# One list of rows per expert, and results added into the output by 39 indirect DMAs

## The chip, the cores and the metric

The kernel runs on one core of a Trainium2 chip. The time is device microseconds (us) of one execution, the median of several. PE is TensorE, DVE is VectorE, ACT is ScalarE, POOL is GpSimd, SP is SyncE, which here only issues DMAs. A "q" behind a name (SPq) is that engine's instruction queue.

## The reference, cut to what matters

All tensors are float32: x is (4, 512, 512), the context (4, 1024, 512), so there are 2048 tokens. First a gated linear attention, then a mixture of 8 experts in which each token takes its best two.

```python
x = x + xattn(layernorm(x), ctx, Wq, Wg, bg, Wkv, Wo)
x = x + ffn(layernorm(x), Wr, We, be)

def ffn(x, Wr, We, be):
    logits = einsum('bsd,de->bse', x, Wr)
    w, sel = top_k(logits, 2)
    w = softmax(w)
    gate = einsum('bsk,bske->bse', w, one_hot(sel, 8))
    out = 0
    for e in range(8):
        out = out + gate[..., e:e+1] * (x @ We[e] + be[e])
    return out
```

## The kernel before, in words

Every engine has its own program; semaphores order them. Every product of two float32 matrices is made of three float32r passes (`three`, L1105: high by high, high by low, low by high), 12 matmuls for 128 rows by 512 by 512.

**Attention.** Batches b = 0 to 3 go one after the other through `queries(b)` and `keys(b + 1, b)`, whose orders are the lists KEYS and QUERIES (L233 to L249). The router's work of batch b (transposes "z", logits "L", ranks "K") is spread over the keys of b + 1. `residual` writes x2 = x + attention, and SP stores x2 of batches 0 to 2 in DRAM (`store_x2`). The normalised rows are scattered by POOL (`scatter`, L490) with two indirect DMAs of 128 rows into xs, one region per expert.

**Groups and tiles.** There are two groups of tokens, batches 0 to 2 and batch 3, each with its own regions, its own plan and its own padding of the last tile of each expert. A tile is 128 rows of one expert. Group 0 has 31 tiles and group 1 has 15, always 46; tiles beyond the real ones repeat the last. `plan` (L957) works out for each tile its expert and first row.

**A tile.** SP loads the rows (`load_tile`, L359, two slots, xs_raw). PE transposes them (`turn_m`, L1173), ACT copies the high part (`high_m`), DVE subtracts for the low part (`low_m`), PE multiplies (`expert`, L1223), DVE adds the expert's bias (`copy_y`, L1021) and ACT stores the tile in the DRAM tensor y. START (L295) fixes the order: the transposes of tile m + 1 stand before the product of tile m, and between the first ten tiles stand the router's steps of batch 3. The split weights of experts 1 to 7 are loaded from DRAM by SP, 2 MB each (`load_halves`); those of 4 to 7 come when attention gives the space back.

**The end.** When all tiles of a group are stored, POOL gathers for each 128 tokens their two rows of y (`gather`, L602), DVE multiplies them by the router's weights and adds them to x2 (`combine`, L1028), and ACT stores the result. Twelve combines run between the tiles of group 1; the four of batch 3 come after the last tile.

## Time and profile before

| | us |
|---|---|
| median of 3 runs | 601.4 (600.34 to 603.24) |
| the profiled execution, its own time | 605.42 |
| its span in the profile | 603.9 |
| PE busy in it | 546.0 |

The span runs from the first to the last instruction; the execution's own time is 1.52 us more. Start and length of instructions below are in us from the span's start.

### The profile page before, as it was taken

How to read it: one execution, taken by the hardware profiler on the slowest of the kernel's cores; microseconds unless marked ns; L12 is line 12 of the kernel's file. 1: busy time of each engine (PE TensorE's matmuls, PEld its weight loads, DVE VectorE, ACT ScalarE, POOL GpSimd, SP SyncE). 2: the span in 40 equal slices, each digit the busy share in tenths (PEclk: the TensorE clock that was granted, in tenths of full speed). 3: DMA queues.
4: the chain of work that ended last, by engine and by line, in shares of the span. 5: the costliest groups of instructions: out<-in, count | busy, mean ns of one | idle time of the engine just before them, and what ended most of it. 6: DMA issues, size and time to landing. Idle time of an engine off the chain costs nothing.

```text
span 603.9 us, 12871 instructions
## 1 busy us (share of the span) xinstructions
PE 546.0 (90%) x4192; PEld 443.9 (74%) x4193; DVE 323.3 (54%) x857; ACT 187.8 (31%) x340; POOL 170.9 (28%) x200
## 2 busy tenths in 40 slices
PE   6999999999999999999999999968799999958850
PEld 4778788878778887877887878856577888846640
DVE  4573367274357556337737537744466444437643
ACT  5455323434422333532343443321111111111100
POOL 4433453315540403632131430010130000156313
PEclk9999999999999999999999999998899999989885
DMA  8912533613541433363062258599566579589946
GB/s 280 363 39 106 174 140 112 238 71 125 192 170 40 162 118 106 144 199 112 0 245 71 79 198 316 198 384 415 189 216 187 163 236 296 160 266 314 380 172 188
DMA packets 44478, 114.18 MB, mean 189 GB/s; under 512 B 5008, under 2 KB 5008, under 8 KB 43536
## 3 DMA queue, kind: packets, MB, share of 16 engines
q1 hardware_dynamic: 24240, 57.43, 27.7%
q0 software_dynamic: 11264, 39.85, 18.9%
q10 hardware_dynamic: 8928, 16.26, 7.1%
q8 instruction: 32, 0.52, 0.4%
q14 instruction: 14, 0.11, 0.1%
HBM read 66.86 MB, written 46.66 MB: 188 GB/s over the span
## 4 chain that ended last, share of the span: by engine, by line
PE 82%; DMA 7%; issue 4%; DVE 3%; another core or an unknown queue 1%; ACT 1%; POOL 1%; SPq 0%; POOLq 0%; DVEq 0%; ACTq 0%
PE pj L1110 23%; PE pj L1112 22%; PE pj L1111 22%; PE tp L1102 5%; DMA khat<-xs 5%; PE tp L1177 3%; PE pj L1197 2%; PE kvb L1169 2%; PE pj L1119 1%; DMA wraw<-in_L_xattn_Wkv_dram 1%; DMA num<-y,gidx 1%; DVE R L809 1%; DVE R L818 1%; ACT R L648 0%
## 5 line engine op out<-in xcount | busy, mean ns | idle before, releaser
L1110 PE MATMUL pj<-R 128*128 128x512 f32 x448 | 184.4, 412 | 4.9 <-DVE R L818 4.3
L1112 PE MATMUL pj<-R 128*128 128x512 f32 x448 | 176.6, 394 | 0.0
L1111 PE MATMUL pj<-R 128*128 128x512 f32 x448 | 175.8, 392 | 0.0
L1110 PEld LDWEIGHTS pj<-R 128*128 128x128 f32 x448 | 84.9, 189 | 21.6 <-DVE R L818 4.5
L1112 PEld LDWEIGHTS pj<-R 128*128 128x128 f32 x448 | 84.6, 189 | 19.1
L1111 PEld LDWEIGHTS pj<-R 128*128 128x128 f32 x448 | 85.1, 190 | 15.2
L1110 PE MATMUL pj<-R,aux 128*128 x184 | 78.7, 428 | 9.5 <-DVE aux L822 6.6
L1111 PE MATMUL pj<-R,aux 128*128 x184 | 73.5, 399 | 0.0
L1112 PE MATMUL pj<-R,aux 128*128 x184 | 73.5, 399 | 0.0
L728 ACT CAST aux<-tp 128x512 fp32r<-128x512 f32 x46 | 26.9, 586 | 128.8 <-PE tp L1177 101.9
L818 DVE TENSOR_TENSOR R<-tp,R 128x512 fp32r<-128x512 f32 x64 | 43.8, 684 | 21.2 <-ACT R L648 21.2
L883 DVE SCALAR_TENSOR_TENSOR khat<-buf,khat 128x512 f32<-128x512 f32 x32 | 25.1, 784 | 53.6 <-ACT buf L687 47.2
L1110 PEld LDWEIGHTS pj<-R,aux 128*128 128x128 f32 x184 | 35.9, 195 | 18.7 <-issue 12.6
L495 POOL DMA_INDIRECT xs<-normed,xidx x16 | 15.9, 992 | 100.4 <-DVE xidx L871 97.9
L608 POOL DMA_INDIRECT qhat<-y,gidx x16 | 16.0, 997 | 98.8 <-issue 78.7
L502 POOL TENSOR_TENSOR rstd<-rstd,mhalf 128x1 f32<-128x1 f32 (+1 forms) x20 | 13.4, 669 | 104.9 <-DVE rstd L836 104.8
L822 DVE TENSOR_TENSOR aux<-tp,aux 128x512 fp32r<-128x512 f32 x46 | 31.7, 689 | 19.6 <-ACT aux L728 17.7
L1112 PEld LDWEIGHTS pj<-R,aux 128*128 128x128 f32 x184 | 35.7, 194 | 7.9
L1177 PE MATMUL tp<-ident,khat 128*128 128x128 f32 x184 | 28.9, 281 | 13.3 <-DMA khat<-xs 13.2
L1111 PEld LDWEIGHTS pj<-R,aux 128*128 128x128 f32 x184 | 36.1, 196 | 6.1
L648 ACT CAST R<-tp 128x512 fp32r<-128x512 f32 x64 | 37.7, 589 | 8.5 <-PE tp L1102 8.0
L1177 PEld LDWEIGHTS tp<-ident,khat 128*128 128x128 f32 x184 | 22.6, 143 | 19.1 <-DMA khat<-xs 11.8
(159 smaller groups left out, 677.0 us busy)
## 6 DMA issues: line engine op xcount, KB each, us to landing
we_halves<-aux POOLq DMA_DIRECT2D x14, 1024.0 KB, 5.1
R<-we_halves SPq DMA_DIRECT2D x7, 2048.0 KB, 11.1
khat<-xs SPq DMA_DIRECT2D x46, 256.0 KB
buf<-in_ctx_dram SPq DMA_DIRECT2D x15, 512.0 KB, 4.2
wraw<-in_L_ffn_We_dram POOLq DMA_DIRECT2D x14, 512.0 KB, 6.7
y<-kvbd ACTq DMA_DIRECT2D x23, 256.0 KB
y<-zeros ACTq DMA_DIRECT2D x23, 256.0 KB
wraw<-in_x_dram SPq DMA_DIRECT2D x4, 1024.0 KB, 8.1
```

The source lines that it names most:

```text
L495: nc.gpsimd.indirect_dma_start(out=xs_dram[g][:, :], out_offset=bass.IndirectOffsetOnAxis(ap=xidx[:, t, j:j + 1], axis=0), in_=xn[t], in_o ...
L608: nc.gpsimd.indirect_dma_start(out=yg[slot][j], out_offset=None, in_=y_dram[g][:, :], in_offset=bass.IndirectOffsetOnAxis(ap=gidx[:, slot, ...
L648: nc.scalar.copy(dst, src).then_inc(SEMS["h_" + kind], 1)
L728: nc.scalar.copy(xsT_hi[:, slot, :, :], tp[slot][:, :, :]).then_inc(MOE["h_m"], 1)
L818: nc.vector.tensor_tensor(lo, tp_bank("l_" + kind, i)[:, :, :], hi.bitcast(F32), ALU.subtract).then_inc(SEMS["l_" + kind], 1)
L822: nc.vector.tensor_tensor(xsT_lo[:, slot, :, :], tp[slot][:, :, :], xsT_hi[:, slot, :, :].bitcast(F32), ALU.subtract).then_inc(MOE["l_m"], 1)
L883: nc.vector.scalar_tensor_tensor(khat[:, i % 2, :], expk[:, i % 2, :], 1.0, khat[:, i % 2, :], ALU.min, ALU.add).then_inc(SEMS["khat"], 1)
L1102: last = nc.tensor.transpose(bank[:, k, :], src[:, k * P:(k + 1) * P], ident[:, :])
L1110: nc.tensor.matmul(bank[:, :], s_hi(k), m_hi(k), start=(k == 0), stop=False)
L1111: nc.tensor.matmul(bank[:, :], s_hi(k), m_lo(k), start=False, stop=False)
L1112: last = nc.tensor.matmul(bank[:, :], s_lo(k), m_hi(k), start=False, stop=(k == KT - 1))
L1177: last = nc.tensor.transpose(tp[slot][:, k, :], xs_raw[:, slot, k * P:(k + 1) * P], ident[:, :])
```

## The change

- One group: xs has one region per expert for all 2048 tokens. A row has 528 elements: 512 values, 8 gates (the router's weight for each expert, 0 for those not chosen), the token's number and a flag for padding.
- 39 tiles in all. The first M0 = 17 are full tiles of batches 0 to 2 in the order of experts (`plan_full`); the other 22 (`plan_rest`) are first tiles that are not needed, which point to four spare blocks of zero rows, and then the remaining tiles, again by expert. The trip count is always 39.
- No y in DRAM, no gathers, no combines. x2 of all four batches is stored in the output itself. Each tile's result gets its bias on DVE, is multiplied by the gate on ACT (`scale_y`), and POOL adds its 128 rows to the output with one indirect DMA with compute_op add (`add_rows`). There are four result buffers, as many as adds can be in flight.
- Two experts' tiles can hold the same token, tiles of one expert cannot. `tile_alone` is 16 for the first tile of an expert's run (and for tile 17) and 0 for the others; it is added to the values that `add_rows` waits for. With 16 the three adds before must have landed, with 0 only those from which the buffers were taken over.
- Padding rows point to tokens of the first 256 which the expert doesn't have (`mark_pads`, `find_pads`, PE step "C"), with values and gates of 0.
- Tile loads have four slots instead of two. SP loads the halves of an expert one after the other, each after the one before has landed. The biases are loaded in part by ACT.
- The loops over tiles, and DVE's loop over batches, are written out.

```diff
-    GROUP_TILES = ((B - 1) * TT, TT)
-    TILES = [2 * n + E - 1 for n in GROUP_TILES]
+    M0 = (2 * (B - 1) * L - E * (P - 1) + P - 1) // P
+    M_ALL = PAIRS // P + E - 1
+    XS, YS = 4, 4
...
+            def load_tile(m):
+                row = sp.value_load(tile_row[0:1, m:m + 1], min_val=0, max_val=E * ROWS + (YS - 1) * P)
+                if m >= XS:
+                    sp.wait_ge(MOE["t_m"], mth(m - XS))
+                    sp.wait_ge(paid, m - XS + 1)
+                sp.dma_start(xs_raw[:, m % XS, :], xs_dram[bass.ds(row, P), :]).then_inc(xs_loaded[m % XS], 16)
             def load_halves(e):
+                sp.wait_ge(wx_stored, 16 * 2 * e)
+                sp.wait_ge(we_ready, 16 * e)
+                sp.dma_start(R[:, 2 * e:2 * e + 2, :, :].rearrange("p a k d -> p (a k d)").bitcast(F32), wx_dram[e, :, :]).then_inc(we_ready, 16)
...
             sp.wait_ge(planned, 1)
-            sp.wait_ge(zeroed, 1)
-            with sp.Fori(0, E) as e:
-                pad(0, e, zeros[:, :])
             for t in range(TT):
                 sp.wait_ge(scattered[t], 32 * (B - 1))
-            load_tile(0, 0, 0)
-            load_tile(0, 1, 1)
-            sp.wait_ge(SEMS["qhat"], nth("qhat", B - 1, G - 1))
-            for e in range(E):
-                sp.dma_start(be_all[:, e, :], be[e:e + 1, :].broadcast_to((P, D))).then_inc(be_loaded, 16)
+            for m in range(XS):
+                load_tile(m)
             sp.wait_ge(SEMS["g"], nth("g", B - 1, TT - 1))
             load_halves(4)
             load_halves(5)
-            load_tile(0, 2, 0)
+            load_tile(XS)
+            store_x2(B - 1)
             sp.wait_ge(SEMS["wo"], nth("wo", B - 1, TT - 1))
-            load_tile(0, 3, 1)
             load_halves(6)
-            load_tile(0, 4, 0)
+            load_tile(XS + 1)
             load_halves(7)
...
+            def add_rows(m):
+                slot = m % YS
+                pool.wait_ge(y_scaled, m + 1)
+                if m >= 1:
+                    alone = pool.value_load(tile_alone[0:1, m:m + 1], min_val=0, max_val=16)
+                    for d in range(1, min(m, YS - 1) + 1):
+                        pool.wait_ge(added[(m - d) % YS], alone + 16 * ((m - d) // YS + 1))
+                nc.gpsimd.indirect_dma_start(out=out_rows[:, :], out_offset=bass.IndirectOffsetOnAxis(ap=out_idx[:, m % (2 * YS):m % (2 * YS) + 1], axis=0),
+                                             in_=y_sb[slot], in_offset=None, compute_op=ALU.add).then_inc(added[slot], 16)
...
+            def scale_y(m):
+                act.wait_ge(MOE["y_copied"], mth(m))
+                nc.scalar.activation(y_sb[m % YS], y_sb[m % YS], ACT.Identity, scale=w_sel[:, m % (2 * YS):m % (2 * YS) + 1]).then_inc(y_scaled, 1)
...
+            def pay(m):
+                e = dve.value_load(tile_expert[0:1, m:m + 1], min_val=0, max_val=E - 1)
+                nc.vector.tensor_scalar(w_sel[:, n:n + 1], row[:, bass.ds(e + GATES, 1)], 1.0, None, ALU.mult)
+                nc.vector.scalar_tensor_tensor(out_idx[:, n:n + 1], pad_token[:, bass.ds(e, 1)], row[:, PADDED:PADDED + 1],
+                                               row[:, TOKEN:TOKEN + 1], ALU.mult, ALU.add).then_inc(paid, 1)
+            def copy_y(m):
                 dve.wait_ge(MOE["m_done"], mth(m))
+                if m >= YS:
+                    dve.wait_ge(added[m % YS], 16 * (m // YS + 1))
+                nc.vector.tensor_tensor(y_sb[m % YS], pj[m % 2][:, :], be_all[:, bass.ds(chosen[m], 1), :].rearrange("p a d -> p (a d)"), ALU.add)
```

`plan_rest` runs in three parts after copy_y of tiles 9, 10 and 11: 14, 13 and 7 DVE operations, each waiting for the one before; the arrays over tiles and experts have 176 elements. `mark_pads` follows after tiles 12 to 14 with 6, 8 and 8 operations. On PE, step "C" after tile 15 is 16 matmuls with one column each.

## Rows read from the trace of the kernel before

**Rows 1.** The page: busy us of each engine, share, instructions.
```profile
PE 546.0 (90%) x4192; PEld 443.9 (74%) x4193; DVE 323.3 (54%) x857; ACT 187.8 (31%) x340; POOL 170.9 (28%) x200
```
**Rows 2.** Windows: start:end length, busy us (instructions) per engine, clock, DMA share, GB/s.
```profile
397.70:451.20 53.50, 41.30 (x337) 31.77 (x336) 25.66 (x104) 9.68 (x20) 7.75 (x10) 0.90 0.78 302
465.00:485.00 20.00, 20.00 (x104) 16.69 (x103) 8.90 (x13) 3.83 (x7) 0.00 (x0) 1.00 0.51 157
529.00:543.00 14.00, 7.82 (x39) 6.08 (x38) 4.99 (x9) 1.21 (x3) 7.97 (x8) 0.87 0.83 273
543.00:583.00 40.00, 35.02 (x152) 27.50 (x150) 27.74 (x49) 5.25 (x9) 14.87 (x14) 0.92 0.87 309
583.00:603.90 20.90, 0.00 (x0) 0.00 (x0) 6.91 (x11) 0.00 (x0) 8.37 (x8) 0.52 0.57 176
```
**Rows 3.** Chain that ended last, in order of time: start, us, what.
```profile
395.29 14.66 DMA khat<-xs
416.47 10.52 DMA khat<-xs
468.25 0.44 PE tp L1177 x4
471.43 0.44 PE tp L1177 x4
534.58 6.08 another core or an unknown queue
550.94 7.76 DMA khat<-xs
582.48 2.19 DMA y<-zeros
595.13 4.64 DMA num<-y,gidx
```
**Rows 4.** Timeline of SP's issues, from 387 to 395.
```profile
387.00 1.91 SPq L363 DMA_DIRECT2D khat<-xs  x2
393.45 1.07 SPq L376 DMA_DIRECT2D R<-we_halves  x2
```
**Rows 5.** Timeline of PE: transposes of tiles 1 and 2; wait before a product.
```profile
397.68 0.60 PE L1177 MATMUL tp<-ident,khat 128*128 128x128 f32 x4
409.99 1.11 PE L1177 MATMUL tp<-ident,khat 128*128 128x128 f32 x4 [8.09 <-DMA khat<-xs]
462.06 0.49 PE L1110 MATMUL pj<-R,aux 128*128 x1 [0.50 <-DVE aux L822]
```
**Rows 6.** Timeline of DVE: plan of group 1, its first and last operations.
```profile
455.31 0.16 DVE L970 SCALAR_TENSOR_TENSOR pad_row<-iota,run 128x8 int32<-128x8 f32 x1
456.73 0.69 DVE L822 TENSOR_TENSOR aux<-tp,aux 128x512 fp32r<-128x512 f32 x1
458.95 0.28 DVE L984 TENSOR_TENSOR qhat<-tile_t,tb 128x120 f32<-128x120 f32 x1
461.13 0.69 DVE L822 TENSOR_TENSOR aux<-tp,aux 128x512 fp32r<-128x512 f32 x1
```
**Rows 7.** Groups by line: names, shapes, count, busy us, mean ns of one.
```profile
L728 ACT CAST aux<-tp 128x512 fp32r<-128x512 f32 x46 | 26.9, 586 | 128.8 <-PE tp L1177 101.9 <-remote 10.3 <-issue 9.2
L658 ACT ACTIVATE normed<-gate,shift,rstd 128x512 f32<-128x512 f32 x8 | 6.5, 816 | 7.8 <-POOL shift L503 7.8
L1119 PE MATMUL pj<-wr_sb,qhat 128*32 128x8 f32 x512 | 7.0, 179 | 0.0
```
**Rows 8.** Timeline of POOL and DVE: gathers of the first combines, and at the end.
```profile
527.68 0.97 POOL L608 DMA_INDIRECT qhat<-y,gidx  x1 [0.30 <-issue]
532.87 0.75 DVE L1032 SCALAR_TENSOR_TENSOR wraw<-qhat,wts,wraw 128x512 f32 x1 [1.63 <-DMA qhat<-y,gidx]
586.85 0.95 POOL L608 DMA_INDIRECT qhat<-y,gidx  x1 [0.30 <-issue]
```
**Rows 9.** The page's DMA issues: KB each, us to landing.
```profile
R<-we_halves SPq DMA_DIRECT2D x7, 2048.0 KB, 11.1
```

More of the change, by code:

```diff
@@ L297, in xattn_moe_kernel @@
         START += [("K", "", 1)] + tiles(6) + [("L", "", 3)] + tiles(7) + [("K", "", 2)] + tiles(8) + [("K", "", 3)]
-        START += tiles(9) + tiles(10) + tiles(11) + tiles(12)
-        LOOP1 = 13
-        N_COMB = GROUP_TILES[0]
-        LOOP2 = M_ALL - N_COMB
-        assert (FIRST[1] - LOOP1) % 2 == 0 and N_COMB == 12 and LOOP2 % 2 == 0 and LOOP2 > FIRST[1]
-        def res_tile(c):
-            return x2r[:, bass.ds(c, 1), :].rearrange("p a d -> p (a d)")
+        for m in range(9, M_ALL):
+            START += tiles(m) + ([("C", "", 0)] if m == M0 - 2 else [])
+        START.remove(("T", "m", M_ALL))
         block = stack.enter_context(nc.Block())
@@ L598, in _ @@
-            halves_in(7)
-            for t in range(TT):
-                scatter(1, last, t)
-            def gather(g, c, slot):
-                pool.wait_ge(gidx_done, c + 1)
-                pool.wait_ge(combined, c + 1)
-                passed()
-                for j in range(2):
-                    nc.gpsimd.indirect_dma_start(out=yg[slot][j], out_offset=None, in_=y_dram[g][:, :],
-                                                 in_offset=bass.IndirectOffsetOnAxis(ap=gidx[:, slot, j:j + 1], axis=0)).then_inc(gathered[slot], 16)
@@ L628, in _ @@
+            for step, kind, i in START:
+                if step == "M":
+                    if i == M0 + 2:
+                        pool.wait_ge(planned, 2)
+                    if i >= 2:
+                        add_rows(i - 2)
+                elif step == "K":
+                    scatter(last, i)
+            add_rows(M_ALL - 2)
+            add_rows(M_ALL - 1)
+            for s in range(YS):
+                pool.wait_ge(added[s], 16 * ((M_ALL - 1 - s) // YS + 2))
         @block.scalar
@@ L998, in plan @@
-                link(nc.vector.tensor_reduce(ys, tok, AX_X, ALU.add))
-                nc.vector.scalar_tensor_tensor(ys, ys, float(P), rank[:, q0:q0 + N, :].rearrange("p q j -> p (q j)"), ALU.mult, ALU.add).then_inc(planned, 1)
-                dve.wait_ge(planned, g + 1)
+                nc.vector.tensor_scalar(tile_expert[:, m0:m0 + T], tile_e[:, 0:T], 0.0, None, ALU.max)
+                link(nc.vector.tensor_tensor(more, big, over(nt[:, 0:E], T), ALU.mult))
+                link(nc.vector.tensor_reduce(tile_b[:, 0:T], more, AX_X, ALU.add))
@@ new lines, in mark_pads @@
+            def mark_pads():
+                tokens = token[:, :].rearrange("p (t e) -> p t e", e=1).broadcast_to((P, 2, E))
+                link(nc.vector.tensor_scalar(early_run[:, :], early_run[:, :], -1.0, float(2 * P), ALU.mult, ALU.add))
+                link(nc.vector.tensor_tensor(member_place[:, :, :], early[:, :, :], over(early_run[:, :], 2), ALU.add))
+                link(nc.vector.tensor_tensor(early[:, :, :], tokens, early[:, :, :], ALU.subtract))
+                link(nc.vector.tensor_tensor(early[:, :, :], early[:, :, :], member_place[:, :, :], ALU.subtract))
+                link(nc.vector.scalar_tensor_tensor(list_place[:, :, :], early_members[:, :, :], 0.0, early[:, :, :], ALU.is_equal, ALU.mult))
+                link(nc.vector.tensor_tensor(list_place[:, :, :], list_place[:, :, :], member_place[:, :, :], ALU.add))
+                dve.wait_ge(x2_stored, 16 * B + 16)
+                yield
+                for t in range(2):
+                    for e in range(E):
+                        last = nc.vector.tensor_scalar(marks[:, t, e, :], place_p[:, :], list_place[:, t, e:e + 1], None, ALU.is_equal)
+                    last.then_inc(pads_marked, 1)
+                    yield
@@ L1042, in _ @@
                     low_m(i, i % 2)
+                    pay(i)
                 elif step == "M":
-                    copy_y(i, i % 2, i // 2)
+                    copy_y(i)
+                    if 9 <= i < 12:
+                        next(planning, None)
+                    if 12 <= i < 15:
+                        next(marking, None)
                 elif step == "L":
@@ L1047, in _ @@
                 elif step == "K":
[L1048 to L1076 removed]
+                    rank_two(LAST, i, pj[2 + i % 2])
+                elif step == "C":
+                    find_pads(pj[2])
         @block.tensor
```

496 lines of the change are left out of this document (228 added, 268 removed).

## The prediction, made before the changed kernel was run

> **What bounds the kernel now.** I read the page's busy times first, then windows, the chain of waits in order of time, and last the timelines of the stretches where the chain leaves PE. PE is busy for 546 of 603.9 us and no other engine for more than 323 [rows 1], so time is won only where PE has less to do or waits less. In the tile stage the chain returns to the transposes every 3.18 us (468.25 to 471.43) [rows 3]: 0.45 for the transposes, 2.73 for 12 products, PE busy throughout at full clock [rows 2]. The stage is a whole: from 397.68, where tile 1 is turned [rows 5], PE works until DVE takes the last tile at 581.8, 184.1 us later. Its work there is 45 x 3.18 + 2.73 = 145.8 for the tiles and some 5 for the router: four transposes like those of [rows 5] at 0.60, four logits steps at 7.0 / 16 = 0.44 [rows 7], and ranks, put at 0.2 each. So 33.3 us of it are not work, and the reader should see where they lie. Early, two tile loads of 256 KB take 14.66 and 10.52 us in the chain [rows 3], because each stands behind halves of 2 MB on SP's queue that were issued just before [rows 4]; PE's clock falls to a mean of 0.90 there [rows 2]. Nine tiles from 397.7 to 451.2 should cost 28.6 + 5 and cost 53.5: 19.9 lost. Late, at 534.58 the chain names an unknown source for 6.08 us, just where ACT, DVE and POOL enter their next loop round, and at 550.94 a tile load takes 7.76 beside gathers [rows 3]; the windows from 529 to 583 have a clock of 0.87 and 0.92 [rows 2]. That is most of the other 13. After the last product comes a tail of 22 us without PE: store, eight gathers one behind the other, a last landing of 4.64, two combines, a store [rows 2, 3].
>
> **The change, part by part.** The sum is made against the profiled execution: span 603.9, and 1.52 around it.
>
> *Seven tiles fewer.* 46 becomes 39: 7 x 3.18 = 22.3 us off PE. The same three-pass product stays. From 397.68: 38 x 3.18 + 2.73 = 123.6, router 5.0, step C 16 one-column products and a wait, 0.8 (nearest row: a logits step of 32, 0.44; bound 0.2 to 2). That makes 129.4, or 527.1. I assume that attention before it runs as now: DVE gains one small operation in `pick_two` and loses one in `rank_two`, under PE's cover; the written out batch loop could give back a us or two at loop edges, which I put at 0 (bound -3 to +2).
>
> *Early loads.* Tiles 0 to 3 are loaded when the plan is ready, some 15 us before the halves of expert 4, since the eight padding stores and their wait are gone. What is late next? Halves 4 can go at 387 instead of 393.45, since no bias loads stand before them [rows 4]. Each pair of halves now waits for the one before; with 7 us each (2 MB at the 302 GB/s of the first window [rows 2]) to 11.1 (the median to landing [rows 9]) halves 7 lands between 415 and 431. Tile 4 lands behind halves 5, tile 5 behind 6, tile 6 behind 7. PE turns tile 4 at about 410, tile 5 at 413, tile 6 at 417. So something like 0 to 14 us is left of the 19.9. In addition SP now stores 1 MB of x2 there and ACT's bias loads come late (the last at about 402), for which copy_y(0) waits, and all of DVE behind it. I take 4.
>
> *Planning on DVE.* Before, 6 and 9 linked operations (455.31 to 456.73 and 458.70 to 461.13) cost PE 0.50 once [rows 5, 6]. Now there are 14, 13 and 7, those over all tiles of 176 elements where 120 took 0.28 [rows 6]: about 3.1, 3.8 and 1.8 us. DVE's own work per tile is two passes of 0.6 and now two small operations and a register load, 1.9 of 3.18, so three tiles take it 14.4 us against 9.5. With a slack of 0.7 this stalls PE by some 4 (bound 1 to 6). The marks behind tiles 12 to 14 are 1 to 1.5 us each and fit.
>
> *The adds.* They are the part that the trace doesn't show. ACT's `scale_y`, 0.82 like the activation in [rows 7], and `high_m`, 0.59, are 1.4 of 3.18: hidden. POOL needs about 0.96 for an indirect DMA and spaces them by 1.25 [rows 8]. y's stores and the gathers of [rows 3] go away. Open is L, the time from an add's issue to its landing. From below: a direct store of 256 KB lands in 2.19 [rows 3]. From above: the slowest 256 KB load beside other traffic, 14.66 [rows 3]. Nearest: a gather, 4.64 at the end [rows 3] and 532.87 - 527.68 = 5.2 under load [rows 8]. An add reads its target and writes it back, so a gather and then a write is 4.64 + 2.19 = 6.8 if they don't overlap. I take L = 6. DMA has room: a load and a store per tile make a share of 0.51 [rows 2]; a second read beside it should give 0.7 to 0.9.
>
> What L costs follows from the waits. The routing is fixed by the inputs; worked out with the reference, the tiles by expert are 3, 2, 3, 2, 2, 2, 3 in the first 17 (experts 0 to 6), then four unneeded ones, then 1, 2, 2, 3, 2, 3, 2, 3. No expert has more than 112 of the first 256 tokens, so no further tile waits. Within a run of n tiles the adds follow 1.25 apart if POOL is behind, between runs one whole L passes. The last eight runs thus take 8 L + 10 x 1.25 at least, against 18 x 3.18 = 57.2 us of PE; an add can go 2.1 us after its product. Counted from tile 21, whose add itself waits for tile 20's, the last landing is 9 L - 42.6 us after the unstalled end of PE; counted over all 16 runs and with the early and planning losses, 16 L - 104. At least it is L + 2.1. The larger counts; whether it shows as PE waiting for a result buffer (copy_y waits for the add four back) or as tail is the same. For L = 5 it is 7.1, for 6 11.4, for 7 20.4, for 8 29.4, for 10 56.
>
> *Tail.* So the 22 us become 11.4, and 0.6 for the end of the program. I allow 2 for clock and issue losses behind the stalls above (the late ones of [rows 3] lose their cause, gathers and loop rounds; bound 0 to 6).
>
> Sum: 527.1 + 4 + 4 + 2 + 11.4 + 0.6 = 549.1 span, 550.6 execution against 605.4, that is 54.8 less. The profiled execution is 4.0 above the median of the runs; taken from 601.4, this leaves 546.6 us.
>
> **The rivals.**
>
> A. *An add is no slower than a gather*, L = 4.7: the chain between experts vanishes and the floor of 6.8 counts, 4.6 less: 542. For it: reading the target overlaps with the data read. Against it: the chip must have the target's value before it can write. The gather row gives 4.64 with nothing else running [rows 3]. The Trainium skill, page "DMA: Bandwidth & Descriptors", section "Anatomy of one DMA — SWDGE (gpsimd) path", gives 2.0 us plus bytes at 436 GB/s, an estimate of 2.6 for 256 KB; the page "Collectives: The Full Stack", section "The bandwidth ceiling: the fold count and why AG ≠ RS ≠ AR", says that an add in the DMA costs two source reads, so half the rate, an estimate of 3.2, and with POOL's 0.96 4.2. By these the sum would be 542 too. This trace's gather is a us above the same estimate without the second read, so I lean to the longer side.
>
> B. *Adds are slow under load*, L = 8: the chain of expert changes sets the end, 18 more: 565. For it: loads beside software gathers took 7.76 [rows 3]. Against it: that was beside a gather every 1.7 us, now there is one in 3.18. PE would be seen waiting for copy_y, on an add.
>
> C. *The early jam stays.* The bytes in front of tiles 4 to 6 are the same 8 MB and 1 MB more, and the serial halves add a landing each. If 20 us are lost as now instead of 4: 563. Against it: four tiles in hand are 13 us of work.
>
> D. *Slower than before.* L above 10.6: then max(9 L - 42.6, 16 L - 104) is over 65 and eats all 54.8. At L = 11.5 the time is 546.6 + 80 - 11.4 = 615. The place is the wait for `added` in `add_rows`, at each change of expert. It can also come from more waits than I count: were every add to wait for the one before, 39 x 6 + 2.1 - 134.6 = 101 us would follow, 636. For it: nothing here shows an add; 128 rows of 2 KB, 8 on each of 16 queues, each read and written back in turn at 1 us or more would do it. Against it: gathers show no such cost per row.
>
> E. *It doesn't do what it says*: the early and late gains are real but PE's tiles grow, since each load has 3% more bytes and DMA is near full. PE has four tiles in hand, so I give this no time of its own.
>
> **How the numbers follow.** Forecast (L between 5 and 7) 0.50, A 0.12, B 0.14, C 0.10, D 0.11, and 0.03 that what is gained and lost comes within 0.5% of nothing, about what a measurement of this kernel can tell from no change. The first four are faster: 0.86; slower 0.11. The predicted time is 547. The forecast's own range is 537 to 558. Ends for 8 in 10: below, A with no losses early and in planning, 542 - 8 = 534; above, it takes in B and C and L up to about 9 (40.3, 29 more: 576), with the other bounds half used 10 more: 586.
>
> **What would show it.** Right: 39 x 16 products and transposes' worth of tiles; a cadence of 3.18; from the last product to the end 7 to 13 us; no wait of PE above 5 us near 395 to 430; PE waits of 1 to 2 us on DVE's plan after tiles 9 to 11; POOL idle at 15 places on the add before. Wrong: PE waiting on DVE's copy, DVE on an add (L too small), or tile loads of 10 us in the chain (C). A landing far from 6 moves the sum most: each us above 6 costs 9, above 8.8 16.

## The result: 3% faster, where 9% were forecast

The changed kernel took 584.2 us (median of 4 runs, 582.0 to 584.9), the kernel before 601.4 beside it: ratio 0.9705, 95% interval 0.967 to 0.974. The forecast was 546.6 with a range of 534 to 586 for 8 in 10, and of 537 to 558 if an add lands 5 to 7 us after its issue. The time lies 2 us from the upper end of the wide range and outside the narrow one, and the saving is 17 us in place of 55. In two later comparisons the unedited kernel gave 0.9695 (0.962 to 0.977) and 0.9705 (0.965 to 0.976).

The page of the changed kernel, its busy times and busy tenths, and the two groups of the adds:

```profile
span 582.5 us, 11999 instructions
PE 524.0 (90%) x4096; PEld 424.8 (73%) x4096; DVE 302.5 (52%) x912; ACT 209.8 (36%) x372; POOL 203.2 (35%) x228
...
PE   5999999999999999999999999998878787988950
...
L597 POOL DMA_INDIRECT out_dram<-khat,out_idx x20 | 31.4, 1569 | 57.3 <-DMA out_dram<-khat,out_idx 17.6
...
L597 POOL DMA_INDIRECT out_dram<-buf,out_idx x19 | 29.7, 1562 | 39.2 <-DMA out_dram<-khat,out_idx 19.3
```

PE lost almost exactly the work that was forecast: 524.0 against 546.0 busy [rows 1] is 22.0 us less, and the sum had 22.3. It is still 90% of the span, so as much waiting is left as before, only of another kind. In the chain of waits from 479 to 485 no product appears at all (start, us, what):

```profile
478.97 5.12 DMA out_dram<-khat,out_idx
484.11 0.03 POOLq L595
484.14 0.04 issue
484.20 0.62 issue
484.83 0.29 POOLq L593
485.12 0.18 POOL out_dram L597
```

An add lands 5.12 us after its issue at 478.97. The next is issued 0.95 later, at 485.04. Within that time POOL's sequencer passes the waits of this add. L593, which reads a flag into a register in 0.29, already belongs to the tile after it. The timeline of POOL from 498 to 522 shows the resulting pattern (in brackets: idle before it, and what ended that):

```profile
498.77 1.55 POOL L597 DMA_INDIRECT out_dram<-buf,out_idx  x1 [0.30 <-issue]
500.63 1.55 POOL L597 DMA_INDIRECT out_dram<-khat,out_idx  x1 [0.30 <-issue]
508.04 1.55 POOL L597 DMA_INDIRECT out_dram<-khat,out_idx  x1 [5.86 <-DMA out_dram<-khat,out_idx]
513.84 1.55 POOL L597 DMA_INDIRECT out_dram<-buf,out_idx  x1 [4.25 <-DMA out_dram<-khat,out_idx]
515.70 1.55 POOL L597 DMA_INDIRECT out_dram<-buf,out_idx  x1 [0.30 <-issue]
521.73 1.55 POOL L597 DMA_INDIRECT out_dram<-khat,out_idx  x1 [4.48 <-ACT buf L739]
```

Inside an expert's run adds follow 1.86 us apart (1.55 + 0.30). From one expert to the next they are 5.8 to 8.2 apart; over the 13 such steps from tile 7's add on the mean is 6.70. At 521.73 the releaser named is ACT, but that ACT operation scales tile 26; the result of tile 24, which is added here, was scaled by 510.15. The chain has the landing of tile 23's add there, 5.22 us after 515.70. The chain reaches PE by another way: a result buffer comes free only with the add four tiles back, so DVE's copies wait for adds, and PE waits for DVE (five times from 480 to 560, 9.5 us in all). The copies in the timeline:

```profile
513.18 0.69 DVE L1068 TENSOR_TENSOR khat<-pj,wraw 128x512 f32<-128x512 f32 x1 [2.55 <-DMA out_dram<-khat,out_idx]
...
519.58 0.69 DVE L1068 TENSOR_TENSOR buf<-pj,wraw 128x512 f32<-128x512 f32 x1 [4.92 <-DMA out_dram<-buf,out_idx]
...
527.71 0.69 DVE L1068 TENSOR_TENSOR khat<-pj,wraw 128x512 f32<-128x512 f32 x1 [5.10 <-DMA out_dram<-khat,out_idx]
```

Windows of the same kernel (length, busy us of PE, PEld, DVE, ACT, POOL; clock, DMA share, GB/s):

```profile
397.00:426.00 29.00, 22.18 (x206) 17.49 (x205) 14.84 (x62) 9.05 (x17) 7.82 (x9) 0.94 0.97 332
460.00:558.00 98.00, 86.02 (x420) 69.04 (x419) 44.81 (x133) 32.21 (x51) 38.89 (x25) 0.98 0.75 143
563.50:582.50 19.00, 0.00 (x0) 0.00 (x0) 0.69 (x1) 0.72 (x1) 4.65 (x3) 0.59 0.48 62
```

The second row is the middle of the stage: PE idles 12 of 98 us at a DMA share of 0.75; in the kernel before it didn't idle at all from 465 to 485 [rows 2]. The third is the tail, 19 us where 12.0 were forecast and 22 stood before [rows 2]. The first is the early stretch, still busy with transfers (0.97). There the timeline has two waits that the prediction had allowed 4 us for:

```profile
408.44 0.69 DVE L1068 TENSOR_TENSOR khat<-pj,wraw 128x512 f32<-128x512 f32 x1 [7.97 <-DMA wraw<-in_L_ffn_be_dram]
...
409.94 0.79 PE L1120 MATMUL pj<-R,aux 128*128 x1 [3.75 <-DVE aux L792]
...
425.69 0.66 PE L1187 MATMUL tp<-ident,buf 128*128 128x128 f32 x4 [3.07 <-DMA buf<-xs]
```

The biases' load lands at 408.4 and holds up the first result copy; tile 6 is turned at 425.69, where about 417.3 would have been due without a wait (an estimate: 397.36 and five steps of 4.0, tiles with a router's step between them).

### The profile page after: what moved, and what is told of

It reads as the page before. It is cut to its first block, busy times and chain, and to the rows that moved or that the text cites. A ratio compares the mean times of both kernels' runs of the same rounds, so it can differ in the third digit from the quotient of the medians.

```text
span 582.5 us, 11999 instructions
## 1 busy us (share of the span) xinstructions
PE 524.0 (90%) x4096; PEld 424.8 (73%) x4096; DVE 302.5 (52%) x912; ACT 209.8 (36%) x372; POOL 203.2 (35%) x228
## 4 chain that ended last, share of the span: by engine, by line
PE 64%; DMA 21%; issue 6%; POOLq 2%; POOL 2%; DVE 2%; SPq 1%; ACT 1%; ACTq 0%; DVEq 0%
PE pj L1120 18%; PE pj L1122 17%; PE pj L1121 17%; DMA out_dram<-khat,out_idx 7%; PE tp L1112 5%; DMA R<-we_halves 5%; DMA out_dram<-buf,out_idx 4%; DMA wraw<-in_x_dram 3%; PE pj L1207 2%; POOL out_dram L597 2%; PE kvb L1179 2%; DMA buf<-xs 2%; POOLq L593 2%; DMA wraw<-in_L_xattn_Wkv_dram 1%; PE tp L1187 1%
## 5 line engine op out<-in xcount | busy, mean ns | idle before, releaser
L1120 PE MATMUL pj<-R,aux 128*128 x156 | 67.4, 432 | 20.7 <-DVE aux L792 13.3
L1122 PE MATMUL pj<-R,aux 128*128 x156 | 63.6, 408 | 0.0
L1121 PE MATMUL pj<-R,aux 128*128 x156 | 63.1, 405 | 0.0
L856 DVE SCALAR_TENSOR_TENSOR khat<-buf,khat 128x512 f32<-128x512 f32 x32 | 23.1, 721 | 56.5 <-ACT buf L673 56.5
L1120 PEld LDWEIGHTS pj<-R,aux 128*128 128x128 f32 x156 | 30.6, 196 | 29.8 <-issue 24.2
L597 POOL DMA_INDIRECT out_dram<-khat,out_idx x20 | 31.4, 1569 | 57.3 <-DMA out_dram<-khat,out_idx 17.6
L597 POOL DMA_INDIRECT out_dram<-buf,out_idx x19 | 29.7, 1562 | 39.2 <-DMA out_dram<-khat,out_idx 19.3
L490 POOL DMA_INDIRECT xs<-normed,xidx x16 | 17.0, 1061 | 71.9 <-DVE xidx L839 69.5
L670 ACT ACTIVATE khat<-pj 128x512 f32<-128x512 f32 x32 | 19.1, 598 | 53.0 <-PE pj L1122 53.0
L721 ACT CAST aux<-tp 128x512 fp32r<-128x512 f32 x39 | 22.7, 582 | 42.7 <-PE tp L1187 41.4
L677 ACT COPY buf<-pj 128x512 f32<-128x512 f32 x32 | 18.8, 587 | 52.5 <-PE pj L1122 52.5
L533 POOL TENSOR_TENSOR aux<-wraw,aux 128x1024 fp32r<-128x1024 f32 x14 | 36.1, 2581 | 1.2
L1122 PEld LDWEIGHTS pj<-R,aux 128*128 128x128 f32 x156 | 30.6, 196 | 6.9
```

Source lines behind the costliest of these rows:

```text
L533: nc.gpsimd.tensor_tensor(aux[:, 2:4, :], e_raw[:, ks, :], aux[:, 0:2, :].bitcast(F32), ALU.subtract).then_inc(wx_low, 1)
L597: nc.gpsimd.indirect_dma_start(out=out_rows[:, :], out_offset=bass.IndirectOffsetOnAxis(ap=out_idx[:, m % (2 * YS):m % (2 * YS) + 1], axis=0),
L670: nc.scalar.activation(khat[:, i % 2, :], pj_bank("expk", i)[:, :], ACT.Relu)
L677: nc.scalar.copy(vones[:, i % 2, :, 0:HD], pj_bank("v_copied", i)[:, :].rearrange("p (g c) -> p g c", g=HEADS)).then_inc(SEMS["v_copied"], 1)
L721: nc.scalar.copy(xsT_hi[:, slot, :, :], tp[slot][:, :, :]).then_inc(MOE["h_m"], 1)
L856: nc.vector.scalar_tensor_tensor(khat[:, i % 2, :], expk[:, i % 2, :], 1.0, khat[:, i % 2, :], ALU.min, ALU.add).then_inc(SEMS["khat"], 1)
```

## The experiments

"W" in the expectations stands for the theory that the waits between adds set the end, "J" and "I" for rivals that they explain. Each comparison ran on one chip together with the kernel before; its median was 603, 591, 602, 604 and 592 us in the five of them, so ratios of different comparisons are not set against each other by less than 2%, and where they would have to be, the traces are compared. The unedited kernel gave 584.2, 585.7 and 585.2, but only where the kernel before took 601 to 604; the second and the fifth comparison (591 and 592) have no unedited kernel of their own. The two profiles of the unedited kernel made later, w0 and z0, have spans of 578.8 and 584.5: single profiles of one kernel differ by up to 6 us. "Counted from tile 1" means from the start of tile 1's transposes.

### First comparison: what do the waits cost, and what do the early loads?

**x1_own_rows.**
```
-    indirect_dma_start(out=out_rows, out_offset=out_idx[:, m % 8], ..., compute_op=ALU.add)
+    indirect_dma_start(out=own_dram[m], out_offset=own_idx, ..., compute_op=ALU.add)
-    pool.wait_ge(added[(m - d) % YS], alone + 16 * ((m - d) // YS + 1))
+    pool.wait_ge(added[(m - d) % YS], 16 * ((m - d) // YS + 1))
```


> Each tile's add goes to 128 rows of its own in DRAM instead of the output, so no add has to wait for another (the register is still loaded and three semaphores are still waited for, on values that only say that the buffers are free). Left out: the experts' part of the output. Theory W (the chain of adds with its landings at every change of expert sets the end from tile 8 on): PE is free of it, the last product ends near 548 instead of 563, then copy, scale, one landing of 5.5 and 5 us of POOL's last drain: span about 564, 18 less than the changed kernel's 582.5. Rival J (the early jam of tile loads and DVE's planning set the end, the chain only fills what they leave): 580 or more. Rival I (POOL's 1.55 us per add and its register load alone are too much): 575 or more, with POOL busy without gaps.


Measured 565.5 us, ratio 0.940 (0.934 to 0.946), span 560.8: near W's 564, while J (580) and I (575) fell. The waits cost some 20 us (585.2 of w0 less 565.5, or 21.7 between the two spans). The window from 476 to 540 of this kernel, PE busy in all of it, where the changed kernel's PE was busy for 56.6 of these 64 us:

```profile
476.00:540.00 64.00, 64.00 (x321) 52.79 (x320) 34.63 (x81) 24.16 (x41) 31.00 (x20) 1.00 0.89 159
```

POOL's timeline at its end: the add itself is as long as before, and POOL idles only until the next result is there.

```profile
544.78 1.55 POOL L600 DMA_INDIRECT own_rows<-khat,own_idx  x1 [1.65 <-issue]
547.89 1.55 POOL L600 DMA_INDIRECT own_rows<-khat,own_idx  x1 [1.56 <-issue]
550.61 1.55 POOL L600 DMA_INDIRECT own_rows<-buf,own_idx  x1 [1.16 <-issue]
```

But even so its span is 11.7 us above the 549.1 that was forecast for the complete kernel, waits included. So the waits between adds are not the whole miss. From tile 1's transposes to the last product (397.4 to 547.6) it takes 150.2 us, of which PE is busy for 137.4; the forecast had 139.4 in all, with 129.4 of work.

**x2_plain_write.** The same waits, the same rows, but the DMA writes instead of adding, so the result is the last expert's part and not the sum.
```
-    in_=y_sb[slot], in_offset=None, compute_op=ALU.add)
+    in_=y_sb[slot], in_offset=None)
```


> The same indirect DMAs into the output with the same waits, but writing instead of adding; the output is then not the sum. Theory W with an add that is dear: issue falls from 1.55 to about 0.96, the landing from some 5.7 to 4 or less, so the chain of 16 landings and 23 spacings is 16 x 1.7 + 23 x 0.6 = 41 us shorter and PE sets the end again: span 562 to 567. Rival (a landing is a landing, reading the target costs nothing): the landing stays at 5.5 or more, only 14 us of spacing go, span 570 or more.


Measured 564.6, ratio 0.937 (0.931 to 0.942). The group of the line in this kernel (min/median/max ns):

```profile
L597 POOL DMA_INDIRECT out_dram<-khat,out_idx x20: 954/958/1066, 412.1 to 550.5; - x20
L597 POOL DMA_INDIRECT out_dram<-buf,out_idx x19: 956/958/962, 425.7 to 553.1; - x19
```

A write occupies POOL for 0.96, an add for 1.55, and from 500 to 527, where one waits for another's landing, they are issued 3.5 to 3.7 us apart; adds there need 5.8 to 7.4. With writes the waits cost nothing: the kernel is as fast as x1, which has none. What costs is waiting for an *add*.

**x4_order and x5_own_order.** Tile loads stand ahead of the next 2 MB of weights on SP's queue, in x5 together with x1's edit.
```
     load_halves(4)
-    load_halves(5)
     load_tile(XS)
     store_x2(B - 1)
+    load_halves(5)
+    load_tile(XS + 1)
+    load_tile(XS + 2)
...
```


> SP issues each early tile load ahead of the next 2 MB of weights instead of behind it; all bytes and waits stay. Theory W alone, with the chain setting the end: its start moves forward as far as tiles 1 to 8 do, 8 to 12 us, and the span falls to about 572. Rival J (the jam is bandwidth, not place in the queue): tile loads 5 and 6 land as late as before, span within 2 us of 582.5. Rival (the chain was so far behind that an earlier start is given back by slower landings beside the weights' 8 MB): 578 or more, with landings over 7 us in the first ten adds.

> Both: own rows for each add without waits between adds, and tile loads ahead of the weights. Left out: the experts' part of the output. Theory W and J together: PE is bound by its own work from 397 on, 129 us, plus 4 to 8 of the first copy's wait for the biases, 4 of planning, and a tail of 12.5: span about 550. If the order alone or the waits alone explain everything, it is no better than the better of the two other kernels.


Measured 588.8, ratio 0.976 (0.971 to 0.982), and 567.0, ratio 0.9405 (0.936 to 0.946). The gains that theories W and J would give did not come. x4's span of 588.1 is in its last alternative (578 or more), of whose landings over 7 us only one was there: tile 2's add at 427.12 took 8.88. x5 is no better than x1, which was its second alternative. The biases landed at 410.3 in x4 and not at 408.4, DVE stood longer, and tile 6 was turned at 425.75 as before. The order moved the wait from one transfer to another.

### Second comparison: biases, unneeded tiles, the end

**y1_own_bias.** x1, and the biases of experts 4 to 7 are waited for only at tile 5.


> As the kernel whose adds go to rows of their own, and the first bias add waits only for the biases of experts 0 to 3; those of 4 to 7, loaded by ACT from 391 to 401 beside the weights, are waited for at tile 5. Left out: the experts' part of the output. If the wait for the last bias load (2.98 us of PE at 409 and half clock behind it) is a loss of its own: 4 to 5 us less than there, span 556. If the loads of tiles 5 and 6, which stand behind 2 MB each, end the wait anyway: within 1.5 us of 560.8, with the wait on the tile load growing from 3.03 to about 7.


Measured 561.1, ratio 0.949 (0.945 to 0.953), span 559.5 (x1: 560.8). The first add went out at 403.4 in place of 410.0, but tile 6 was turned at 426.9 (425.0), and nothing more than the 1.3 us between the spans came of it.

**y2_skip_unneeded.** The rows of unneeded tiles lie outside the bounds given to the DMA, and tile 17 waits for nobody.
```
+    bounds_check=B * L - 1, oob_is_err=False,
-    link(tensor_tensor(tile_u, tile_u, tile_t, ALU.max))
```


> The four unneeded tiles point beyond the output, where the indirect DMA writes nothing, so tile 17 need not wait for the adds before it. Everything is computed. Theory W (each change of expert costs the chain one landing, about 6.6 from issue to issue instead of 1.85): one such step less is 4.7, and the step after the unneeded ones shrinks since they move no data, 2 to 4 more; span 574 to 577. Rival: the chain has slack there and PE takes over, span 580 or more. If the test of bounds makes POOL's 1.55 us longer, it is slower than 584.


Measured 583.3, ratio 0.987 (0.983 to 0.991). From tile 14's add to the last it takes 81.9 us in place of 86.6, as expected, but tile 14's add itself went out at 489.4 and not 485.0.

**y3_sp_waits_last.** SP waits for the last adds instead of POOL.
```
-    for s in range(YS): pool.wait_ge(added[s], ...)
+    for s in range(YS): sp.wait_ge(added[s], ...)
```


> SP instead of POOL waits for the last four adds, so POOL comes to its final drain while they are under way. In the kernel before, POOL's drain ended 2.1 us after the last landing, in the changed one 5.2 after it, of which 4.9 are the drain itself. If the drain overlaps with the landing: 3 us less, span 579.5. If it starts its 4.9 us when the last DMA has landed: no change.


Measured 584.0, ratio 0.986 (0.982 to 0.990). From the last add's issue to the end it is 7.9 us in place of 10.9, but this add went out at 574.6 and not 571.6.

**y4_skip_and_sp.** Both.


> Both edits, everything computed. If they add: 571 to 574 of span, a time of about 574, 1.5 to 2% under the changed kernel. If the skipped tiles give nothing: about 580.


Measured 581.7 (6 runs), ratio 0.983 (0.980 to 0.987), span 580.0. The local gains show in the traces and hardly in the times. Counted from tile 1, tile 14's add goes out after 92.4, 91.3 and 90.5 us in y2, y3 and y4, and after 87.0 to 88.3 in the three profiles of the unedited kernel. Neither edit changes when an add before tile 14's may go, so why this stretch is 2 to 5 us longer here isn't shown, and gains of this size can't be judged by these times.

### Third comparison: the weights later

**z0_after** is the unedited kernel.


> The changed kernel itself, unedited, so that the others of this call stand beside it on one chip: span about 582.5; last product near 563, last add issued near 571.6.


Measured 585.7; tile 6 turned at 426.5.

**z1_late_weights** and **z2_own_late** load the weights of experts 5, 6 and 7 behind tile loads 6, 9 and 12; z2 has x1's edit too. **z4_all_edits** is z1 with y4's edits.
```
-    load_halves(5)
...
     load_tile(XS + 1)
     load_tile(XS + 2)
+    load_halves(5)
     load_tile(XS + 3)
...
```


> SP loads the weights of experts 5, 6 and 7 (2 MB each, first used at tiles 12, 14 and 36) only behind the loads of tiles 6, 9 and 12. Bytes in all and waits are the same. If the early loss is bandwidth (8 MB beside the tile loads, the biases and the last store of x2): tile 6 is turned near 418 instead of 425.7, the chain of adds starts as much earlier and, being what sets the end, ends 7 to 9 us earlier: span 574 to 576. Rival (the chain's start is set by POOL's scatters and DVE's ranking, not by the loads): 580 or more.

> Adds to rows of their own without waits between adds, and the late weights. Left out: the experts' part of the output. Nothing but PE's work, DVE's planning (4.2) and the ranking (2) is left before the tail: last product near 538 to 541, span 552 to 554. If late weights only move the jam (tiles 12 to 14 wait for their weights): 558 or more.

> Late weights, unneeded tiles that write nothing, SP waiting for the last adds; everything computed. If the three gains add (8, 4.7 and 3): 15 us under the changed kernel, span near 567. If the chain falls to PE's pace in places, so that gains overlap: 570.


Measured 589.2, ratio 0.9725 (0.964 to 0.981); 562.6, ratio 0.932 (0.926 to 0.938); 583.6, ratio 0.966 (0.959 to 0.972). z1 turned tile 6 at 417.71, 8.8 us earlier, and was no faster; z2 fell on its second alternative and is near x1. POOL's timeline of z1:

```profile
419.12 1.60 POOL L602 DMA_INDIRECT out_dram<-buf,out_idx  x1 [0.30 <-issue]
431.97 1.58 POOL L602 DMA_INDIRECT out_dram<-buf,out_idx  x1 [11.25 <-DMA out_dram<-buf,out_idx]
433.86 0.99 POOL L495 DMA_INDIRECT xs<-normed,xidx  x1 [0.30 <-issue]
435.15 0.98 POOL L495 DMA_INDIRECT xs<-normed,xidx  x1 [0.30 <-issue]
436.44 1.61 POOL L602 DMA_INDIRECT out_dram<-khat,out_idx  x1 [0.30 <-issue]
447.55 1.58 POOL L602 DMA_INDIRECT out_dram<-khat,out_idx  x1 [9.51 <-DMA out_dram<-khat,out_idx]
```

Two adds, issued at 419.12 and 436.44 around loads of 2 MB (SP issues them at 418.51 and 436.60), hold up the next for 12.9 and 11.1 us; in w1 below, where these loads are nearly empty, the same two steps take 5.7 and 6.0. The jam that PE was spared fell on the chain of adds.

This also says why z4's three edits came to nothing. Against z0, run beside it, the skipped waits win 5.1 us from tile 14's add to the last and SP's wait 3.0 at the end. But from tile 1's transposes to tile 14's add z4 takes 95.0 us, like z1, and z0 88.3: the late weights lose 6.8 of the 8.1.

### Fourth comparison: bytes taken away, waits added

**w0_after** is the unedited kernel.


> The changed kernel once more, as the base of the three others of this comparison: ratio to the kernel before about 0.970, span 582 to 585, tile 6 turned at 426.


Measured 585.2, ratio 0.9705 (0.965 to 0.976).

**w1_few_bytes** and **w2_own_few**: the loads of the weights of experts 4 to 7 are cut to 256 bytes per partition; w2 has x1's edit too.
```
+    n = 2 * KT * D if e < 4 else 64
-    sp.dma_start(R[...].bitcast(F32), wx_dram[e, :, :])
+    sp.dma_start(R[...].bitcast(F32)[:, 0:n], wx_dram[e, :, 0:n])
```


> The loads of the weights of experts 4 to 7 copy 256 bytes per partition in place of 16 KB (the products of these experts are left without their weights); queue order and waits are unchanged. By the theory that these bytes cause the early loss (8.4 us at tiles 4 to 6) and that the adds' chain, 6.6 us per change of expert and 1.85 per add, sets the end from the first add on: tile 6 turned near 417.5, first add near 403 to 406, last add 6 to 8 us earlier, span 574 to 577. By the rival that the chain is bound again by the plan, the marks and the loads of tiles 14 to 17 in the middle, whatever came before: span 580 or more.

> Few bytes as in w1_few_bytes, and each add goes to 128 rows of its own without a wait for other adds (the combination of the experts' parts is left out). If the weights' bytes are the early loss and PE is the bound behind it: 7 to 8 us less than x1_own_rows, span 552 to 554. If DVE's planning, the stores and the loads of tiles 13 to 17 take it back, as they did in z2_own_late: 559 to 562.


Measured 577.5, ratio 0.957 (0.952 to 0.961), and 561.5, ratio 0.930 (0.9255 to 0.935). Where the adds wait for each other, the bytes cost 8 us. Where they don't, they cost at most 4 (561.5 against x1's 565.5 in another comparison), and by the traces 1: from tile 1's transposes to the last add it takes 152.2 us against 153.2 in x1, although tile 6 comes 6 us earlier by this count. PE's waits from 397 to 480 in w2 (total us, times, longest):

```profile
PE pj L1124 <- DVE aux L796: 8.3, 3, 4.2
PE pj L1124 <- issue: 2.8, 5, 1.2
```

Without the jam PE waits for DVE instead, which does the router's steps and the planning there. The last product ends at 547.6 in x1 and 548.1 in w2, where the forecast had 537.1. That this is near what PE and DVE allow is argued and not shown: no run takes DVE's steps away.

**w3_all_wait.** Every add waits for the one before.
```
-    pool.wait_ge(added[(m - d) % YS], alone + 16 * ((m - d) // YS + 1))
+    pool.wait_ge(added[(m - d) % YS], 16 + 16 * ((m - d) // YS + 1))
```


> Every add waits for the add before it, also inside an expert's run; everything is computed. If a step with a wait costs 6.6 us and one without 1.85, as the trace of the changed kernel has it: 38 steps of 6.6 behind a first add at about 411 put the last add at 662 and the span at 672 (ratio to before about 1.115). If adds of one expert share queues and engines so that waiting costs them less than an add of another expert (landing nearer 5 than 6): 38 x 5.9, last add 635, span 645. The recorded prediction's figure for this case was 636.


Measured 661.0, ratio 1.096 (1.090 to 1.101), between the two expectations: 38 steps in 235.8 us are 6.21 each. The line's landings in this kernel:

```profile
L597 POOL DMA_INDIRECT out_dram<-khat,out_idx x20: 1549/1549/1673, 411.4 to 641.7; - x20
...
DMA to landing us min/median/max: 4.5/5.3/6.0
```

The exemption inside an expert's run, the second half of the change's description, is therefore worth 76 us (661.0 - 585.2), and it is what turns a loss of 10% into a gain of 3%.

### Fifth comparison: what stands between the adds

In all these traces POOL's queue had something that no experiment had touched. The changed kernel from 441 to 458:

```profile
442.25 1.58 POOL L597 DMA_INDIRECT out_dram<-khat,out_idx  x1 [4.17 <-DMA out_dram<-khat,out_idx]
444.14 0.99 POOL L490 DMA_INDIRECT xs<-num,xidx  x1 [0.30 <-issue]
445.44 0.98 POOL L490 DMA_INDIRECT xs<-num,xidx  x1 [0.30 <-issue]
446.73 1.61 POOL L597 DMA_INDIRECT out_dram<-buf,out_idx  x1 [0.30 <-issue]
448.65 0.98 POOL L490 DMA_INDIRECT xs<-num,xidx  x1 [0.30 <-issue]
449.93 0.96 POOL L490 DMA_INDIRECT xs<-num,xidx  x1 [0.30 <-issue]
451.20 1.61 POOL L597 DMA_INDIRECT out_dram<-buf,out_idx  x1 [0.30 <-issue]
458.23 1.57 POOL L597 DMA_INDIRECT out_dram<-khat,out_idx  x1 [5.42 <-DMA out_dram<-buf,out_idx]
```

POOL never idles for more than 0.3 us at a time between 442 and 452. The last batch's eight scatters (L490) stand in pairs before the adds of tiles 2, 4, 6 and 7, each inside an expert's run, where the add waits for no other add: four pairs of 2.57 us on the queue. Behind tiles 2, 4, 7 and 9, the last of their runs, POOL waits 4 us and more with nothing to do.

**v1_scatters_in_gaps** moves these four pairs there, and nothing else. **v2_all_with_scatters** adds z4's edits.
```
     if i >= 2:
         add_rows(i - 2)
-elif step == "K":
-    scatter(last, i)
+        if i - 2 in (2, 4, 7, 9):
+            scatter(last, (2, 4, 7, 9).index(i - 2))
```


> The four pairs of scatters of the last batch stand on GpSimd's queue behind the adds of tiles 2, 4, 7 and 9, each the last of an expert's run, where the next add waits 4 us and more anyway; in the changed kernel they stand before the adds of tiles 2, 4, 6 and 7, where none waits. Everything is computed. If the chain of adds sets the end from the first add on, and the scatters are links of it: four pairs of 2.57 us less, add of tile 7 at 441 to 444 in place of 450 to 451, ratio to before about 0.955 (8 to 10 us less than the changed kernel, span 573 to 576). If PE and the loads of tiles 8 to 17 set the pace there (product before the add of tile 8): 2 to 4 us less, ratio 0.965.

> The scatters as in v1, and with them the three edits of z4_all_edits: late weights, rows of unneeded tiles skipped by the bounds check and tile 17 not waiting, SyncE waiting for the last adds. Everything is computed. If the scatters were what kept the three from showing: 4.7 for the skipped waits and 3 for the end below v1, ratio 0.940 to 0.945, span 565 to 568. If an add beside a 2 MB load lands some 5 us later, as the two of tiles 2 and 4 did in z1_late_weights, the late weights give that back: ratio 0.955, no better than v1.


Measured 577.3 (573.0 to 580.3, 6 runs), ratio 0.974 (0.970 to 0.978), and 564.8 (562.4 to 567.5, 6 runs), ratio 0.953 (0.950 to 0.9565). The kernel before took 592.4 on this chip, so the ratios miss the expected ones while the spans, 576.0 and 562.2, meet or beat them. The same stretch in v1:

```profile
440.20 1.54 POOL L597 DMA_INDIRECT out_dram<-buf,out_idx  x1 [1.56 <-issue]
442.05 1.00 POOL L490 DMA_INDIRECT xs<-num,xidx  x1 [0.30 <-issue]
443.35 0.98 POOL L490 DMA_INDIRECT xs<-num,xidx  x1 [0.30 <-issue]
445.75 1.61 POOL L597 DMA_INDIRECT out_dram<-khat,out_idx  x1 [1.42 <-ACT khat L739]
```

Tile 7's add goes out at 440.20. Counted from tile 1's transposes (397.36 in the changed kernel, 394.89 here) that is 45.3 us in place of 53.8: 8.5 earlier. Not all of it is scatters: with the first pair goes a wait of 4.48 us for DVE's ranks, which had stood before tile 2's add. 4.4 us are lost again behind tile 7, so that the last add goes out after 170.1 us and not 174.3; in the other two profiles of the unedited kernel it is 171.4 and 174.7. That v1 alone is faster than the changed kernel is not shown: its ratio is no lower (0.974 against 0.9705), and its times, 7 to 8 us below the three medians of the unedited kernel, come from a comparison in which the kernel before was faster too.

The better pair is z4 and v2, which differ in the place of the scatters alone, though they ran in different comparisons: 583.6 and 564.8, with ratios of 0.966 (0.959 to 0.972) and 0.953 (0.950 to 0.9565). Counted from tile 1, the last add goes out after 176.4 us in z4 and after 159.0 in v2, and tile 7's add is already 19.5 earlier. The steps behind the adds of tiles 2 and 4 take 7.1 and 9.5 us in v2, and 12.3 and 12.2 in z4. So with late weights the place of the scatters matters most. How much of the 17.4 us is the scatters' own time, and how much that these adds no longer fall beside the loads, no run tells apart.

v2 against v1 is, in the same comparison: 564.8 / 577.3 = 0.978. Both turn tile 1 at the same moment (394.89 and 395.00), and the 13.8 us between their spans can be read off: tile 7's add 4.4 earlier (late weights), tile 7 to 14 0.4 later, tile 14 to the last 7.1 less (the skipped waits), the end 2.8 less (SP's wait). The page of v2:

```profile
span 562.2 us, 12036 instructions
...
PE 519.8 (92%) x4096; PEld 422.9 (75%) x4096; DVE 303.4 (54%) x910; ACT 208.8 (37%) x372; POOL 204.7 (36%) x228
```

v2 computes everything and beats both kernels. Its ratio to the kernel before is 0.953, and the changed kernel's interval (0.967 to 0.974) lies above all of v2's (0.950 to 0.9565), although it was measured where the kernel before was slower (601.4 against 592.4), which lowers a ratio.

## Why the prediction missed, step by step

*Seven tiles fewer: right.* 22.0 us of PE work against 22.3, and a cadence of 3.2 where nothing waits.

*Early loads, 4 us: too little.* Tile 6 came some 8.4 late. That the serial halves jam there was seen, and that ACT's bias load comes late too (408.4, not 402); rival C had the mechanism. w1 puts the price of these bytes at 8 us of the end, and w2 shows that little of it would be had if the adds didn't wait.

*Planning, 4 us: right.* The three parts took 3.28, 3.57 and 1.89 us (forecast 3.1, 3.8, 1.8), and PE stood 1.69 and 2.36 behind the first two.

*What is left of the waiting on PE's side: too little, by 10.8.* Of the 33.3 us that were not work the forecast kept 10: 4 for loads, 4 for planning, 2 for clock and issue. x1, where no add waits for another, still has 20.8: in its 150.2 us PE idles for 12.8, and its work takes 137.4 in place of 129.4, at a mean granted clock of 0.94 up to 480. The kernel before had this too: from 397.7 to 582 PE was busy for 161.1 us, where the prediction counted 150.8 of work, so some 10 of its 33.3 were slow work and not waits. The 2 us for clock and issue were the term with the least behind it. In w2, without the weights' bytes, 19.7 are left.

*The adds: the step that failed most.* The number everything was hung on, L = 6, was close: 4.9 to 7.4 in the trace, 5.3 the median in w3. The formula around it was wrong. It was max(9 L - 42.6, 16 L - 104). At L = 6 the first branch governs, 11.4: it says that the chain binds only from tile 20's add on, and the second, -8, that the first 20 tiles leave 19.4 us of slack. In numbers of the trace: the forecast has tile 20's add at 548.5 - 9 x 6 - 10 x 1.25 = 482.0; it went out at 500.63, 18.6 late. The second branch, taken back through 15 changes and 23 steps of 1.25, starts from a first add at 404.4. What used up the slack, by the issue times of the adds (rows are rounded; unrounded they sum to the 18.6):

| term, first add to tile 20's | forecast | measured | late |
|---|---|---|---|
| first add issued | 404.4 | 410.7 | 6.4 |
| 7 changes of expert | 7 x 6 | 47.9 | 5.9 |
| 5 steps of tiles 1, 2, 4, 6, 7 | 5 x 1.25 | 27.2 | 21.0 |
| 8 other steps inside runs | 8 x 1.25 | 14.9 | 4.9 |
| slack | | | -19.4 |

The third row is the largest: 10.3 of its 21.0 us are the eight scatters, which stand on POOL's queue in plain sight in the code and which the part on the adds never counted; 4.8 are POOL's waits for DVE's ranks ahead of the first two pairs, 2.6 the wait for tile 1's result, and the rest POOL's own time for an add. "Within a run the adds follow 1.25 apart if POOL is behind" took the spacing of gathers [rows 8]; POOL needs 1.55 for an add, so 1.86. And "between runs one whole L passes" left out the 0.95 from a landing to the next issue. From tile 20 on the same two terms cost 10.5 more: 8 changes in 52.5 against 48, 10 steps in 18.5 against 12.5.

The table says when the adds went out, not that the adds alone made it late. The profile's chain stays on PE until 466.4 and passes to the adds only from tile 11's, at 468.90. In x1, without waits between adds, tile 20's add still goes out 96.1 us after tile 1's transposes; it is 103.3 in the changed kernel, and the forecast had 84.3. So 7.2 us of this stretch are the waits, and 11.8 come without them: early loads, ranks, scatters, planning, clock. x1 doesn't part these, since it keeps the scatters where they were.

*Tail.* POOL passes its last wait at 577.1, 5.4 after the last add's issue, 0.6 less than L. The end of the program, put at 0.6, took 5.5: POOL's closing drain begins behind this wait (577.4) and lasts 4.89. In the kernel before it began at 590.4, while the last gathers and stores were under way, and hid behind them. y3 and v2 give about 3 us of it back.

The sum: 18.6 + 10.5 - 0.6 + 4.9 = 33.4, and the span is 582.5 against a forecast 549.1, also 33.4 more. The experiment cuts the same 33.4 another way. Without waits between adds the forecast's own terms give 537.1 + 8.1 + 0.6 = 545.8; x1 has 560.8. So 15.0 us remain without any wait between adds: the 10.8 on PE's side and most of the rest in the end of the program. The waits were to cost 3.3 on top and cost 21.7, 18.4 more.

*The rivals.* B (slow adds, 565) named the sign that came, PE held up through the result copies on an add, for a different reason: not L but what is added to it at each step. C (the early jam stays, 563) is half of it: tile 6 was late as it says, and w1 gives 8 us for it, not 16. That the time came within the wide range is no merit of the sum: its upper end was made for slow adds (L up to 9), and L was near 6. D's figure for waiting at every add was 636; w3 shows 661. A is out: it needs landings at 4.7 and no chain between experts, and in the trace an add lands 4.9 to 7.4 us after its issue, where the gather took 4.64 [rows 3], and costs POOL 1.55 in place of 0.96. The rule of the Trainium skill quoted there (page "Collectives: The Full Stack", section "The bandwidth ceiling: the fold count and why AG ≠ RS ≠ AR") is stated for the bandwidth of a collective's reduce step, whose add needs two source reads. x2 agrees in direction (steps of 3.5 to 3.7 us for writes, 5.8 to 7.4 for adds), but the 4.2 us estimated from it for one add's landing were too few against a median of 5.3 in w3.

What stays open: why the steps behind tile 7 grew by 4.4 us in v1 (the steps behind the adds of tiles 16, 20 and 21 grew most, to 7.95, 8.39 and 7.54 us from 6.31, 7.41 and 5.80), what makes up the 20.8 us on PE's side one by one, and which part of an add's landing is the reading of its target.

## What to carry to other kernels

Where work is strung on one in-order queue, write that queue's whole list first, with everything that stands between the links, and count slack from its first link; a formula made of the links alone gave 19 us of slack that weren't there. Put work that is independent of the chain where the queue waits anyway: tile 7's add went out 8.5 us earlier by that alone, though it took the late weights too for the time to show it. Where waits on another engine (33.3 us here) are said to vanish, price what stays, the slower products included, before anything is built on the difference. And when sound edits show in the trace and not in the time, measure every other stretch against an unedited kernel run beside them: in z4 one of the three lost in front what the other two won behind.

## What the runs showed of the chip

- An indirect DMA of 128 rows of 2 KB occupies POOL for 0.96 us as a write and 1.55 as an add; the add lands 4.5 to 6.0 us after its issue where every add waits (w3), and around loads of 2 MB the next add followed only 11 to 13 us later (z1), against 5.7 and 6.0 where these loads carry next to nothing (w1).
- Where the bounds check leaves out all 128 rows, the add costs POOL the same 1.55 us (y2, tiles 17 to 20, issued 1.85 to 3.2 us apart).
- Where POOL waits last for its own DMAs, its closing drain of 4.89 us begins after the landing, and the program ends 5.5 us after it (changed kernel). Where SP waits in its place, the drain runs beside the landing, and the last add's issue is 7.9 us from the end in place of 10.9 (y3).
- From a landing to the issue of the add that waited for it POOL takes 0.95 us (changed kernel, 484.09 to 485.04). Reading a flag into a register takes its sequencer 0.29.
